# Software-pipelined dense FFN of layer 0, and the weight statistics moved from VectorE to ScalarE and GpSimd, in a two-layer transformer kernel on 8 cores

## The reference, cut to what matters

```
layer 0 attn: xi = layernorm(xn); 16 heads of 128; window of 256 keys + 16 global keys; softmax; @ Wo.T; + xn
layer 0 ffn : h = gelu(xn @ W1.T)                    # 2048 -> 8192, 16 blocks of 512
              h = h * mask[token, block]             # top 4 of 16 blocks by a router
              y = h @ W2.T                           # 8192 -> 2048
layer 1 attn: decayed linear attention (SiLU q, k, v; RMS norm; sigmoid gate)
layer 1 ffn : q(w) = clip(round(w / mean(|w|)), -1, 1)
              y = (sigmoid(x q(w1).T) * (x q(w2).T)) q(w3).T      # 2048 -> 5632 -> 2048
```

## Time and profile before

| what | us |
|---|---|
| time before, median of 2 runs (lowest, highest) | 11254.36 (11039.97, 11468.75) |
| the profiled execution's own time | 11039.97 |
| its span (slowest core, first to last instruction) | 11038.4 |
| spans of the 8 cores | 10986.9 to 11038.4 |
| PE busy / weight loads (PEld) / DVE / ACT / POOL | 6034.0 / 2667.5 / 2925.1 / 1600.4 / 995.1 |

### The profile page before, as it was taken

The page is one execution under the profiler, slowest core; times in us unless marked ns, Lnnn a source line. Parts: engine busy times, 40 slices in busy tenths (PEclk is TensorE's granted clock), DMA queues, the critical chain, the costliest instruction groups (busy, mean ns, idle before and its releaser), DMA issues.

```text
span 11038.4 us, 87872 instructions; the slowest of 8 cores (10986.9 to 11038.4 us)
## 1 busy us (share of the span) xinstructions
PE 6034.0 (55%) x28009; PEld 2667.5 (24%) x28009; DVE 2925.1 (26%) x5558; ACT 1600.4 (14%) x4936; POOL 995.1 (9%) x512
## 2 busy tenths in 40 slices
PE   1455546445444633555556667655545545577776
PEld 1222222122212211222222223222222222233332
DVE  6222221111111134222221000011121121566665
ACT  3122220110011012222202102011121120000000
POOL 0000000000000000000000000000000000344442
PEclk9766668777777766666778889877766768788888
DMA  1322324459744952221245786862111102333332
GB/s 43 63 43 43 51 49 98 90 76 111 102 81 75 105 95 53 43 43 31 46 90 83 79 84 96 80 78 42 31 23 31 31 16 38 90 95 95 96 94 82
DMA packets 1017525, 743.96 MB, mean 67 GB/s; under 512 B 676465, under 2 KB 898546, under 8 KB 1010802
## 3 DMA queue, kind: packets, MB, share of 16 engines
q0 software_dynamic: 885824, 397.12, 30.3%
q1 hardware_dynamic: 69042, 202.78, 5.8%
q10 hardware_dynamic: 62208, 138.44, 4.6%
HBM read 1110.22 MB, written 25.17 MB: 103 GB/s over the span
## 4 chain that ended last, share of the span: by engine, by line
PE 41%; DMA 27%; DVE 16%; issue 8%; ACT 7%; DVEq 1%; ACTq 0%; POOL 0%; POOLq 0%; SPq 0%
PE ps L248 27%; DMA pool<-fw2T 6%; DMA pool<-w2T 6%; DMA pool<-fw3T 4%; PE psTf L257 4%; PE ps L1412 4%; PE ps L737 4%; DMA pool<-fw1T 3%; DVE pool L876 3%; DMA pool<-wqkv 3%; DVE pool L1351 2%; ACT pool L610 2%; ACT pool L272 1%; ACT pool L704 1%; DMA pool<-wvT 1%
## 5 line engine op out<-in xcount | busy, mean ns | idle before, releaser
L248 PE MATMUL ps<-pool 128*128 128x512 bf16 (+2 forms) x16256 | 3658.8, 386 | 1241.2 <-ACT pool L558 371.9
L248 PEld LDWEIGHTS ps<-pool 128*128 128x128 bf16 x16256 | 1582.3, 102 | 3175.0 <-issue 1644.2
L257 PE MATMUL psTf<-pool 128*128 128x128 bf16 (+1 forms) x3872 | 562.8, 262 | 2590.5 <-DVE pool L708 894.6
L737 PE MATMUL ps<-pool 128*128 128x512 bf16 x4096 | 1028.6, 418 | 643.6 <-DMA pool<-w2T 643.6
L876 DVE TENSOR_REDUCE pool<-pool 128x1 f32<-128x704 f32 (+1 forms) x432 | 347.5, 804 | 2735.3 <-DMA pool<-fw3T 1102.1
L257 PEld LDWEIGHTS psTf<-pool 128*128 128x128 bf16 (+1 forms) x3872 | 310.1, 108 | 3003.5 <-issue 2959.3
L737 PEld LDWEIGHTS ps<-pool 128*128 128x128 bf16 x4096 | 428.2, 106 | 1224.8 <-issue 834.1
L1354 POOL TENSOR_TENSOR pool<-pool 128x1024 bf16<-128x1024 bf16 x264 | 616.1, 2334 | 849.7 <-DVE pool L1351 775.2
L272 ACT CAST pool<-psTf 128x128 bf16<-128x128 f32 (+1 forms) x2720 | 522.1, 274 | 1068.1 <-PE psTf L257 780.4
L1351 DVE TENSOR_SCALAR pool<-pool 128x1024 bf16<-128x1024 f32 x264 | 537.6, 2036 | 0.0
L1412 PE MATMUL ps<-pool 128*128 128x512 bf16 x1408 | 394.2, 444 | 81.7 <-ACT pool L313 36.2
(11 more groups left out here) (131 smaller groups left out, 3181.7 us busy)
## 6 DMA issues: line engine op xcount, KB each, us to landing
pool<-w1T POOLq DMA_DIRECT2D x64, 2048.0 KB, 15.8
pool<-w2T POOLq DMA_DIRECT2D x64, 2048.0 KB, 25.9
pool<-fw1T ACTq DMA_DIRECT2D x128, 352.0 KB, 3.1
pool<-fw2T ACTq DMA_DIRECT2D x128, 352.0 KB, 5.1
pool<-fw3T ACTq DMA_DIRECT2D x176, 256.0 KB, 2.8
pool<-fw1T SPq DMA_DIRECT2D x88, 512.0 KB, 4.0
pool<-fw2T SPq DMA_DIRECT2D x88, 512.0 KB, 3.8
pool<-fw3T SPq DMA_DIRECT2D x88, 512.0 KB, 3.6
```

The source lines that it names most:

```text
L248: p=(f == nk - 1): E.matmul(o, lt, rh, start=s, stop=p),
L257: E.matmul(o, s, self.identb, start=True, stop=True), dd)
L737: E.matmul(bk, lt, rh, start=s, stop=p),
```

## The change

In stage W1 the matmuls of tile k+1 are recorded ahead of the Gelu, mask and transposes of tile k. `gel`, `gmb` and `yts` get two buffers each, in bf16 where `gel` and `yts` were f32. The load of block ibc+2 waits for the last matmul of block ibc in place of its last transpose copy, and is recorded, with the `gamma.step(3)` ahead of it, inside `em_mm` behind the fourth tile's matmuls. The first two loads stand ahead of everything. Stage W2 is changed in the same way, and its transposes are of bf16. In `GammaStream.step` the sum of |w| is an ACT activation (Abs with an accumulated output, written in place), and the addition to `gacc` is POOL's. That function serves all callers, those in attention and wo too, whose own code is not touched.

```diff
+        def w1_stream(ibc):
+            if ibc < 16:
+                b = ibc % 2
+                dd = [w1_tok[b], mm_done.get(ibc - 2)]
+                w1_tok[b] = kb.stream_cast(w1c[b], kb.inp["w1T0"], D,
+                                           ibc * 512, (ibc + 1) * 512, dd)
+        def em_mm(k):
...
+            if t4 == 3:
+                mm_done[ibc] = tm
+                if getattr(kb, "gamma", None):
+                    kb.gamma.step(3)
+                w1_stream(ibc + 2)
+            mmq[k] = (bi, bk, tm)
+        w1_stream(0)
+        w1_stream(1)
+        em_mm(0)
+        for k in range(len(seq)):
+            if k + 1 < len(seq):
+                em_mm(k + 1)
...
+            tg = kb.act(lambda E, bk=bk, o=gel: E.activation(
+                out=o, in_=bk, func=AF.Gelu), [tm, prev_tmk_[p2]])
...
+        def w2_mm(f):
...
+            tm_done[f] = tm
+            if getattr(kb, "gamma", None):
+                kb.gamma.step(3)
+            w2_stream(f + 2)
+            w2q[f] = (bi, bk, tm)
...
-                [:, half * 4:half * 4 + 4, :], [tev])
-            f_done[f] = last
+                [:, half * 4:half * 4 + 4, :], [tev], fp32=False)
...
-            tr = kb.dve(lambda E, a=self.wst[b][:, 0:piece]: E.reduce_sum(
-                self.pcolg, a, axis=AX.X, apply_absolute_value=True),
+            tr = kb.act(lambda E, a=self.wst[b][:, 0:piece]: E.activation(
+                out=a, in_=a, func=AF.Abs, accum_out=self.pcolg),
                 [tl, self.prev_add])
-            self.prev_add = kb.dve(
+            self.prev_add = kb.pool_op(
                 lambda E, o=kb.gacc[:, t:t + 1]: E.tensor_add(o, o, self.pcolg),
                 [tr])
```

More of the change, by code:

```diff
@@ L681, in emit_l0_segment @@
     prog.barrier(exclude=QACT_DOMS)
[L682 to L685, removed]
+    gel_ = [ar.alloc(f"gelE{i}", 512, BF16) for i in range(2)]
+    gmb_ = [ar.alloc(f"gmbE{i}", 512, BF16) for i in range(2)]
+    yts_ = [ar.alloc(f"ytsE{i}", 512, BF16) for i in range(2)]
+    prev_tmk_ = [None, None]
+    prev_tlast_ = [None, None]
     for half in range(2):
@@ L688, in emit_l0_segment @@
         w1_tok = [None, None]
-        ib_done = {}
-        for ibc in range(16):
-            b = ibc % 2
[L692 to L718, removed]
@@ new lines, in emit_l0_segment @@
+        mm_done = {}
+        mmq = {}
+        seq = [(ibc, t4) for ibc in range(16) for t4 in range(4)]
+        def w1_stream(ibc):
[5 more added lines that the diff above has]
+        def em_mm(k):
+            ibc, t4 = seq[k]
+            b = ibc % 2
+            ti = half * 4 + t4
+            bi, bk, bd = kb.bank([w1_tok[b]])
+            tm = kb.mm16(bk, lambda f, ti=ti: xnT[:, f * TOWN + ti * 128:
+                                                  f * TOWN + (ti + 1) * 128],
+                         lambda f, b=b: w1c[b][:, f * 512:(f + 1) * 512], bd)
+            if t4 == 3:
[4 more added lines that the diff above has]
+            mmq[k] = (bi, bk, tm)
@@ L722, in emit_l0_segment, with w2_stream @@
         w2_tok = [None, None]
-        f_done = {}
-        for f in range(16):
-            b = f % 2
[L726 to L730, removed]
+        tm_done = {}
+        w2q = {}
+        def w2_stream(f):
+            if f < 16:
+                b = f % 2
+                dd = [w2_tok[b], tm_done.get(f - 2)]
+                w2_tok[b] = kb.stream_cast(w2c[b], kb.inp["w2T0"], FF0,
+                                           f * 128, (f + 1) * 128, dd)
+        def w2_mm(f):
+            b = f % 2
             bi, bk, bd = kb.bank([w2_tok[b]])
@@ L738, in emit_l0_segment @@
                            bd if it == 0 else ())
-            tev = kb.act(lambda E, bk=bk: E.copy(yts, bk), [tm])
+            tm_done[f] = tm
[3 more added lines that the diff above has]
+            w2q[f] = (bi, bk, tm)
+        w2_stream(0)
+        w2_stream(1)
+        w2_mm(0)
+        for f in range(16):
+            if f + 1 < 16:
+                w2_mm(f + 1)
+            bi, bk, tm = w2q.pop(f)
+            yts = yts_[f % 2]
+            tev = kb.act(lambda E, bk=bk, o=yts: E.copy(o, bk), [tm])
             kb.bank_last[bi] = tev
-            last = kb.tgrp_add(
+            kb.tgrp_add(
                 [yts[:, j * 128:(j + 1) * 128] for j in range(4)],
                 fview(kb.acc, 8, D, f * 128, (f + 1) * 128)
-                [:, half * 4:half * 4 + 4, :], [tev])
-            f_done[f] = last
+                [:, half * 4:half * 4 + 4, :], [tev], fp32=False)
         prog.barrier(exclude=QACT_DOMS)
         ar.free("w2c0", "w2c1")
-    ar.free("hTb", "gel", "gmb", "ytsE", "xnT", "mask_sb")
+    ar.free("hTb", "gelE0", "gelE1", "gmbE0", "gmbE1",
+            "ytsE0", "ytsE1", "xnT", "mask_sb")
     prog.barrier(exclude=QACT_DOMS)
```

16 lines of the change are left out of this document (added).

## The result

The changed kernel is slower: 11818.5 us (median of 13 runs, 11539.9 to 11992.84) against 11351.08 (12 runs, 11013.13 to 11560.68). The ratio is 1.0482 with a 95% interval of 1.0377 to 1.0587: a mean of 11582 us (two executions, 11539.9 and 11624.23) against 11050 (four, 11013.13 to 11109.4). The forecast was 11185 and no change that can be measured. The profiled execution has spans of 11436.3 to 11622.7 us.

What follows compares the result with a forecast made beforehand. No engine was taken to bound the whole span; W2 was bound by weight loads. Attention +629, W1 -487, wo -12 and W2 +15 gave +145 us on 11040: 11185 us, range 11035 to 11430.

Steps and rivals of the forecast that it cites:

- Forecast +629: Attention in P and O: POOL's additions delay each head's weight loads, 18.7 to 23.0 us more a head, +629 us.
- The trip that I made 0.25 us longer: Statistics round trip in attention: Abs, addition on POOL and hand-overs make it 0.25 us longer, between nothing and +2.5.
- Rival D: Attention: a head's loads are not held up, additions come early enough; 10732 us, faster; chance 0.05.
- Rival A: Statistics trips: the addition on POOL costs 0.45 us more than taken, 400 trips, +180 us, 11365; chance 0.20.
- I forecast -487 us: All W1 stages in P and O: pipelined tiles and shorter blocks save 117, 145, 128 and 97 us.
- the 15.9 us of a block that waits for its load: W1 without statistics: two blocks take 31.5 us, bounded by the weight load; 15.9 us taken for one.
- the 29.4 us of a block with statistics: W1 with statistics: a block is a chain of three pieces, 13.9 us, then Gelu, transposes and matmuls; 29.4 us.
- the w1T load of 15.7 us: W1 without statistics: the weight load takes 15.7 us, bounds 14.0 and 16.5, and is what is late next.
- the 18 us that I had named as a sign of being wrong: W1: the prediction is wrong if blocks without statistics stay over 18 us.
- the forecast's +15: W2 in P: pieces nearly fill a chunk's 27 to 28 us and trips are longer; +15 us, bounds -30 and +60.
- Rival C: W2 in O: loads follow each other closer, 402 to 355 us in two stages; 11090 us; chance 0.10.
- rival B: W1 without statistics: dense matmuls run at a lower clock, 3.2 us more a block, +57 us, 11240; chance 0.08.

Runs made afterwards that it cites:

- e3: Changed kernel with step(6), a head's six statistics pieces, recorded behind the head's two weight loads; 10910.57 us.
- e5: Changed kernel with the Abs still on ACT and the addition to gacc back on VectorE; 10999.14 to 11031.42 us, 10677.93 when run again.
- e1: Changed kernel with the statistics' reduction and addition back on VectorE, pipelining kept; 10695.72 us beside 10961.08 and 10970.36 for the kernel before.
- e4: Changed kernel with half of each w1T load, the other half of the buffer zeros; 11492.56 us.
- e11: e8 with the statistics spread: two DMAs at the start, single pieces behind a tile's matmuls; 9722.42 to 9742.61 us, ratio 0.8835 to the kernel before.
- e2: Kernel before with only the statistics moved to ScalarE and GpSimd; 13055.19 us beside 10961.08 and 10970.36 for the kernel before.
- e8: e1 with two result columns, a statistics DMA waiting for the addition of the piece before the last; 10195.86 us against 10970.38 before.
- e12: Changed kernel whose w1T loads in segment O wait for the second tile of the next block; 11853.38 us.

## Why the prediction was right or wrong

**Attention, right.** Forecast +629, measured +669 (again +663), with PE's wait for wqT at 34.8 us where 35 was forecast, and by the mechanism named: POOL's additions ahead of the head's loads (e3, e5). The trip that I made 0.25 us longer did not grow (4.42 us), while the load took 7.3 and not 6.5 us beside the last statistics. Rival D is out. Rival A is out by its price: L919 takes 0.19 us, and POOL starts it 0.29 us behind the Abs (1489.55 to 1489.84). L915 brought no table loads (20 on ACT in either kernel, core 0). Two slips in my working change nothing: it gives 22.1 and not 21.3 us for the start of a group in O (3 us in all), and the 408 trips named with the skill's page on GpSimd should be the 400 of rival A.

**W1, the step that failed.** I forecast -487 us (-117, -145, -128, -97). Measured: -85, -87, -46, -28, a sum of -246, and -266 again. The mechanism held: e1 shows that the pipelining gains, and a tile without statistics took 3.68 us. What failed are the sizes: the 15.9 us of a block that waits for its load, which took 19.4, and with it the 29.4 us of a block with statistics, which took 31, what I put around the blocks, and the base. To part them, the table takes the time from the Gelu of the first block's first tile to that of the last block's (15 blocks) and the rest of the stage (its ends), by the median over the cores. Where the two do not add up to the stage, the medians are to blame.

| | stage, forecast and measured | 15 blocks | ends |
|---|---|---|---|
| P, first | 490, 536 | 441, 468 | 49, 69 |
| P, second | 490, 519 | 441, 461 | 49, 55 |
| O, mixed | 347, 405 | 298, 351 | 49, 56 |
| O, second | 273, 337 | 238, 290 | 35, 46 |

First, the w1T load of 15.7 us. Its rows come from a stage in which a load starts every 21 us. Timeline, changed kernel, O's second W1 stage, core 0:

```profile
7193.04 1.14 POOL L363 DMA_DIRECT2D pool<-w1T  x1 [19.34 <-PE psTf L257]
7194.94 3.61 PE L248 MATMUL ps<-pool 128*128 128x512 bf16 x16 [2.49 <-DMA pool<-w1T]
...
7210.20 1.14 POOL L363 DMA_DIRECT2D pool<-w1T  x1 [16.02 <-PE psTf L257]
...
7215.66 5.95 PE L248 MATMUL ps<-pool 128*128 128x512 bf16 x16 [5.85 <-DMA pool<-w1T]
```

The block at 7215.66 waits for the load issued at 7193.04: 22.6 us. A block took 18.5 to 21.4 us in the mean of a core, 19.4 by the median of these, in place of 15.9: 52 us in the second stage. The blocks without statistics of the mixed stage took 19.7 us, which is 34 us more. That is past the 18 us that I had named as a sign of being wrong. e4 shows that the load is the bound. In e1, whose loads land in 16 to 20 us, the mean block took 17.2 us (16.4 to 18.0) and the stage 297, so that some 20 us of the 52 lie in any kernel with this order, and the rest goes with the changed kernel's longer loads. My bounds of 14.0 and 16.5 were those of one window, and I had written "with all cores loading closer together" and given that 0.1 us.

Second, the statistics in P. Timeline, changed kernel, one block of W1, core 0:

```profile
2306.80 1.18 POOL L363 DMA_DIRECT2D pool<-w1T  x1 [0.38 <-issue]
...
2321.22 0.34 ACTq L217 DMA_DIRECT2D pool<-fw1T  x1
...
2332.45 0.33 ACTq L217 DMA_DIRECT2D pool<-fw2T  x1
...
2336.51 0.58 ACT L727 ACTIVATE pool<-ps 128x512 bf16<-128x512 f32 x1
...
2337.36 1.18 POOL L363 DMA_DIRECT2D pool<-w1T  x1 [0.37 <-issue]
```

Three pieces take 15.3 us (2321.22 to 2336.51) where I took 13.9. The first two trips are 5.6 us each (to the DMAs at 2326.80 and 2332.45). I knew that a head's weight loads stretch the trips and did not carry it over to W1. This block is 30.6 us, not 29.4; on the cores 4 to 7, where w1T landed last (last section), the mean is 31.8 to 32.2. The blocks with statistics cost 27 and 20 us more than forecast in P's two stages, and some 16 in O's mixed one (30.9 us each in place of 27.6).

Third, the ends: 20, 6, 7 and 11 us more than I had put there, some 44 in all. A stage's first block waits for the first of two loads that are asked for together. In O's second stage PE waited 30.2 us for it on core 0, where I had put 15. What lengthened P's first stage was not looked into.

Fourth, the base. The 635 us of P's second stage are core 0's; the median over the cores is 606. And my window of O's mixed stage ran until 6191, 27 us into W2: its last mask multiplication is at 6164. Core 0's first stage was shorter than the median (607 against 621), so that 45 us of the gain in all were read off one core and one wrong edge.

So of the 241 us some 86 are O's blocks that wait for their load, 63 the blocks with statistics, 44 the ends and 45 the base.

**wo and W2.** Wo gave -6 (forecast -12). W2's +54 and, again, +8 include the forecast's +15, and two profiles of before differ by 38. Rival C did not happen in the changed kernel, though O's W2 did take 347 to 353 us a stage in e5 and e11, near its 355.

**The lower clock (rival B).** It did not bind here: in the dense stretch from 7181 to 7192 the granted clock was 1.00 and 16 matmuls took 3.62 us. It appeared in e4, on the cores 0 and 1, in the same stage. Window (the granted clock is the third figure from the end) and timeline of core 0, then a window of core 2:

```profile
6960.00:6972.00 12.00, 12.00 (x55) 5.29 (x53) 1.06 (x3) 2.67 (x11) 0.00 (x0) 0.81 0.39 59
```

```profile
6963.24 4.37 PE L248 MATMUL ps<-pool 128*128 128x512 bf16 x16
```

```profile
7150.00:7180.00 30.00, 29.84 (x162) 14.60 (x163) 2.82 (x8) 10.78 (x42) 1.76 (x2) 1.00 0.49 70
```

16 matmuls take 4.37 us at a granted clock of 0.81, neither of the two levels. The Trainium skill (TensorE: Matmul & The Clock Gate, Seeing it yourself) says that the whole die falls to 1.95 GHz, 0.81 of 2.4, once three of its cores run dense matmuls. This row agrees with the level; the one of the changed kernel shows that it need not come, and e4 that it does not take the whole die: there the clock records of the cores 0 and 1 have 0.81 in the same stretches (6382 to 6719 on both) and those of 2 and 3 have it at other times. With halved loads nothing hides the price: a block took 17.8 and 17.5 us on the cores 0 and 1 and 14.7 on the others, 3 us, as the rival's 3.2 says. Where the load is the bound it is hidden: in e3 most of this stage ran at 0.81, and it took 336 us against the changed kernel's 337.

**The sum.** 669 - 246 - 6 + 54 + 13 is +484 by the stages' medians, against my +145. The slowest core alone gives more: the profiled executions differ by 584 us, the means of the result section by 532. Of the 339 us between the two sums W1 is 241, attention 40 and W2 39. My range ended at 11430 because its upper end was built from attention and rival A; a W1 that gains half was in no rival.

## What to carry to other kernels

Before an operation that waits is moved to a queue that also issues loads, list what stands behind it there in every caller: a 0.19 us addition, six times in a head, made PE wait 35 us where it had waited 14, and in the old loops (e2) the same move cost some 2090 us in all. A load's duration read where loads are sparse is no price for a stage in which they follow each other; take a range from the busiest stretch in the trace, price a block by the mean and not the median (in e1 blocks of 14.7 us and of up to 19.8 alternate), and read stage lengths on several cores. What shortened the serial chain of small transfers here was asking for each one early (e8, e11), not moving its arithmetic.

## What the runs showed that I had not expected

**A load is slower beside one other core's.** In one W1 stage of the changed kernel (P, first) the landing of w1T depends on the core. Tile w1T, window 2300:2600, cores 0 to 7 in order:

```profile
DMA to landing us min/median/max: 15.9/16.6/18.4
DMA to landing us min/median/max: 16.5/17.8/20.0
DMA to landing us min/median/max: 16.0/16.5/21.1
DMA to landing us min/median/max: 15.8/17.2/19.0
DMA to landing us min/median/max: 20.8/22.4/24.5
DMA to landing us min/median/max: 22.1/23.4/24.4
DMA to landing us min/median/max: 22.3/23.7/25.4
DMA to landing us min/median/max: 21.0/22.3/23.9
```

One issue each from the timelines of cores 0, 1, 4 and 5, in this order:

```profile
2306.80 1.18 POOL L363 DMA_DIRECT2D pool<-w1T  x1 [0.38 <-issue]
...
2317.62 1.18 POOL L363 DMA_DIRECT2D pool<-w1T  x1 [0.37 <-issue]
...
2409.39 1.18 POOL L363 DMA_DIRECT2D pool<-w1T  x1 [0.38 <-issue]
...
2409.82 1.18 POOL L363 DMA_DIRECT2D pool<-w1T  x1 [0.38 <-issue]
```

Cores 4 and 5 issue within 0.5 us of each other, cores 0 and 1 some 11 us apart. For every w1T transfer, from its first packet to its landing, I worked out how much of it lay beside a transfer of the other core of its pair (0 and 1, 2 and 3, and so on), of the other pair of the die, and of the other die. This counts each core's time from its own first instruction, as if all started together. A linear fit over P's first W1 stage gives 13.7 us and +7.3 for full overlap with the pair's core, and between -0.2 and +0.5 for a core of the others; it explains 0.80 of the variance (second profile: 13.8, +6.6, 0.79). In O's two W1 stages of the changed kernel the same fit explains only some 0.2, so that it does not account for the load that bound them. In the kernel before the pairs' loads hardly met in that stage (a mean overlap of 0.01), and a transfer took 13.1 us. In e12's last W1 stage the overlap was 0.36, where the changed kernel had 0.80, and the mean transfer fell from 18.3 to 15.3 us. The Trainium skill (HBM Reference, Specifications (TRN2)) says that two cores of a domain share its bandwidth, some 358 GB/s each when both stream. The fit agrees that two share. A block of 2048 x 512 f32 is 4.19 MB, so the fit's 21.0 us would be some 200 GB/s for each, well under the page's figure; what holds these loads there is not shown. This pairing is a correlation over runs and one intervention (e12), not a proof.

**Open: the same instructions at two speeds.** e1's transfers in O's second W1 stage took 15.1 us at an overlap of 0.78, and the changed kernel's 18.3 at 0.80. W2 in O took 347 to 353 us in e5 and e11, and 397 to 427 in all others; both kinds repeated in a second profile, though the stage's instructions are the same. Something about the kernel as a whole decides it, and no run here tells what.
